# One-hot comparisons between the subtraction pieces, two batch tiles of pair products in a row, and the second layer of tile 2 moved ahead of the last pair products

## The reference, cut to what matters

```python
e = jnp.stack([tbl_0[ids[:, 0]], ..., tbl_25[ids[:, 25]]], axis=1)      # 512 x 26 x 128
combined = jnp.concatenate([e, r_dense_x[:, None, :]], axis=1)          # 512 x 27 x 128
interact = jnp.einsum('bfd,bgd->bfg', combined, combined)
z = interact[:, triu_i, triu_j]                                         # 512 x 351
h = jnp.concatenate([z, r_dense_x], axis=1)                             # 512 x 479
h = jnp.maximum(h @ W_top1 + b_top1, 0.0)                               # 512 x 512
h = jnp.maximum(h @ W_top2 + b_top2, 0.0)                               # 512 x 256
y = h @ W_top3                                                          # 512 x 1
```

## Time and profile before

| | |
|---|---|
| median of 3 runs | 109.18 us (109.17 to 109.2) |
| profiled execution | 109.18 us; span from its first to its last instruction 107.4 us |
| granted PE clock | 0.999 of full speed over the span |
| busy share of the span | PE 92%, DVE 74%, ACT 70%, POOL 62% |
| stretch 33.7 to 38.2 us, one turn of the one-hot loop | 4.50 us long: DVE busy 4.50, ACT busy 4.50, PE 4.45 |
| stretch 72.0 to 84.0 us, one batch tile | 12.00 us long: PE busy 12.00, DVE 7.61, ACT 6.42 |
| DMA, mean over the span | 108 GB/s; 343 to 398 GB/s from 18 to 24 us |

### The profile page before, as it was taken

How to read it: one execution, slowest core, us unless ns; L and a number is a source line. 1 busy time by engine, 2 the same in 40 slices (tenths; PEclk the granted TensorE clock), 3 DMA queues, 4 the chain that set the end, 5 groups by cost and what they waited for, 6 DMA issues and landing times.

```text
span 107.4 us, 2605 instructions
## 1 busy us (share of the span) xinstructions
PE 98.5 (92%) x998; PEld 79.0 (74%) x998; DVE 79.8 (74%) x162; ACT 75.0 (70%) x149; POOL 66.3 (62%) x72
## 2 busy tenths in 40 slices
PE   5999899989799999999798978999999989998992
PEld 1356676657467675887478958999999979997991
DVE  6599999999999999999943974588338922685120
ACT  4499999999999999999706842475527732474430
POOL 3777777777777787777877777777777750000000
PEclk9999999999999999999999999999999999999999
DMA  3852749995663636621211221221121220000000
GB/s 46 334 209 58 235 76 372 374 345 113 217 197 101 221 78 218 225 92 49 55 49 49 53 50 49 63 66 49 49 55 49 58 67 3 6 0 0 6 0 1
DMA packets 5200, 11.64 MB, mean 108 GB/s; under 512 B 1979, under 2 KB 2491, under 8 KB 5189
## 3 DMA queue, kind: packets, MB, share of 16 engines
q1 hardware_dynamic: 3120, 7.27, 21.2%
q0 software_dynamic: 2048, 4.20, 14.2%
q10 hardware_dynamic: 20, 0.02, 0.1%
HBM read 11.48 MB, written 0.00 MB: 107 GB/s over the span
## 4 chain that ended last, share of the span: by engine, by line
DVE 46%; PE 44%; issue 6%; ACT 2%; POOL 0%; DVEq 0%; POOLq 0%
DVE onehot L464 22%; PE gram_ps L613 13%; DVE low L476 13%; PE top_ps L678 5%; PE tr_ps L594 5%; PE act_ps L667 4%; PE dve_ps L667 4%; DVE onehot L470 3%; DVE xt L473 2%; PE gram_ps L578 2%; PE top_ps L702 2%; PE tr_ps L653 1%; DVE xt L450 1%; PE dve_ps L626 1%; PE act_ps L626 1%
## 5 line engine op out<-in xcount | busy, mean ns | idle before, releaser
L287 POOL DMA_INDIRECT rows<-table,ids_sb x64 | 65.5, 1023 | 20.8 <-issue 19.2
L578 PE MATMUL gram_ps<-onehot,high 128*128 128x512 f32 x82 | 23.1, 410 | 1.9 <-DVE onehot L464 1.6
L578 PE MATMUL gram_ps<-onehot,low 128*128 128x512 f32 x82 | 22.1, 411 | 0.0
L578 PEld LDWEIGHTS gram_ps<-onehot,high 128*128 128x128 f32 x82 | 14.3, 188 | 8.8 <-DVE onehot L464 5.0
L578 PEld LDWEIGHTS gram_ps<-onehot,low 128*128 128x128 f32 x82 | 15.4, 189 | 3.9
L464 DVE TENSOR_TENSOR onehot<-dve_ps,row_f 128x1024 fp32r<-128x1024 f32 (+1 forms) x10 | 14.4, 1479 | 1.2 <-PE act_ps L554 1.2
L464 DVE TENSOR_TENSOR onehot<-gram_ps,row_f 128x1536 fp32r<-128x1536 f32 (+1 forms) x10 | 14.9, 1531 | 0.0
L613 PE MATMUL gram_ps<-xt 128*58 128x52 f32 x512 | 14.5, 217 | 0.3 <-issue 0.3
L483 DVE COPY gram_sb<-gram_ps 26x208 f32<-26x208 f32 x32 | 12.0, 376 | 3.6 <-PE gram_ps L613 2.4
L613 PEld LDWEIGHTS gram_ps<-xt 128*58 128x58 f32 x512 | 14.0, 133 | 0.9 <-issue 0.5
L385 ACT ACTIVATE onehot<-onehot 128x1344 fp32r<-128x1344 f32 (+1 forms) x10 | 14.3, 1426 | 0.0
(11 more groups left out here) (83 smaller groups left out, 111.7 us busy)
## 6 DMA issues: line engine op xcount, KB each, us to landing
table<-table SPq DMA_DIRECT2D x9, 512.0 KB, 3.6
rows<-table,ids_sb POOLq DMA_INDIRECT x64, 2.9
w1p_sb<-w_pairs SPq DMA_DIRECT2D x1, 768.0 KB
table<-table SPq DMA_DIRECT2D x1, 640.0 KB, 3.8
w_sb<-w SPq DMA_DIRECT2D x1, 512.0 KB
dense_sb<-dense SPq DMA_DIRECT2D x1, 256.0 KB, 5.1
w1d_sb<-w_dense SPq DMA_DIRECT2D x1, 256.0 KB
ids_sb<-ids SPq DMA_DIRECT2D x1, 52.0 KB, 2.0
```

What stands on the lines that cost most here:

```text
L287: pool.indirect_dma_start(rows[:, t, s - 1, :], None, tables[f], bass.IndirectOffsetOnAxis(ids_sb[:, t, f:f + 1], 0)).then_inc(gathered[t] ...
L578: last = pe.matmul(pick_ps[b][:], weights[:, c, :], onehot[:, b, c, :], start=(c == 0 and part == 0), stop=(c == CHUNKS[o] - 1 and part == 1))
```

## The change

1. In the one-hot stage DVE's list is one turn ahead: between the four subtraction pieces of o stand the comparisons of o + 1. The three-chunk comparison is cut in two (`DVE_CHUNKS`), so a turn has one instruction more. The clears of `xt` for tiles 0 and 1 stand ahead of the first comparison, those for tiles 2 and 3 behind the one-hot stage.
2. `spread` from o = 2 on multiplies 10 rows instead of 128; the second of the two reads copies of its operands at partitions 32 to 41 (`select_again`, `ids_again`), which SP makes with two small transfers ahead of the table of o = 2.
3. Tiles 0 to 2 have four banks of four slots. The transposes of tile 0 stand behind the picks of o = 6 and o = 7, two banks of tile 1 behind those of o = 8, and the other two ahead of `gram(0)`.
4. The loop over t is written out: `gram(1)` comes right behind `gram(0)` and half of `dense_part(0)`. The banks of the pair products rotate over all tiles (`n % 3`).
5. `second_layer(2)` stands ahead of `gram(3)`, its two halves around the transpose of the last slot. It stood behind `gram(3)`.

```diff
-DVE_CHUNKS = {8: ((0, 1), (2, 3, 4)), 10: ((0, 1, 2), (3, 4, 5))}
+DVE_CHUNKS = {8: ((0, 1), (2,), (3, 4)), 10: ((0, 1, 2), (3,), (4, 5))}
...
+BANKS = [range(n, n + 4) for n in range(1, NG + 1, 4)]
+LAST_BANKS = BANKS[:-1] + [range(NG - 3, NG), range(NG, NG + 1)]
+BANK_SLOTS = [BANKS] * (TILES - 1) + [LAST_BANKS]
...
             for o, f in enumerate(ONEHOT):
+                if o == TABLES:
+                    sp.wait_ge(select_ready, 1)
+                    sp.dma_start(select_again[SPREAD_AT[1]:SPREAD_ROWS], select[0:NO]).then_inc(spread_again, 16)
+                    sp.wait_ge(ids16_ready, 1)
+                    sp.dma_start(ids_again[SPREAD_AT[1]:SPREAD_ROWS], field_ids16[0:NO]).then_inc(spread_again, 16)
                 if o >= TABLES:
                     sp.wait_ge(low_ready, REST * (o - TABLES + 1))
...
             for o in range(NO):
-                if o == NO - 1:
-                    transposed(0, (0, 1))
                 onehots(o)
...
+                if o == NO - 3:
+                    transposed(0, (1,))
+                if o == NO - 2:
+                    transposed(0, (3,))
...
             dve.tensor_copy(field_ids16[0:NO], field_ids[:]).then_inc(ids16_ready, 1)
+            for t in (0, 1):
+                dve.memset(xt[:, t, :, N_SLOTS:PAD], 0.0).then_inc(pad_zero, 1)
...
-                if o < TILES:
-                    dve.memset(xt[:, o, :, N_SLOTS:PAD], 0.0).then_inc(pad_zero, 1)
...
+            dve.wait_ge(ids_spread, 1)
+            whole_chunks(0, 0)
+            shared_chunk(0)
+            whole_chunks(0, 1)
+            whole_chunks(0, 2)
+            for o in range(NO - 1):
                 dve.wait_ge(high_ready, o + 1)
-                for c in rest_pieces(o):
-                    dve.tensor_tensor(low[:, b, c], table[:, o % TABLES, c], high[:, b, c].bitcast(F32),
-                                      ALU.subtract).then_inc(low_ready, 1)
+                rest(o, 0)
+                dve.wait_ge(ids_spread, o + 2)
+                if o >= 1:
+                    dve.wait_ge(pick_done, o)
+                whole_chunks(o + 1, 0)
+                if o == NO - 3:
+                    transposed(0, (0,))
+                if o == NO - 2:
+                    transposed(0, (2,))
+                rest(o, 1)
+                shared_chunk(o + 1)
+                rest(o, 2)
+                whole_chunks(o + 1, 1)
+                rest(o, 3)
+                whole_chunks(o + 1, 2)
...
+                pe.matmul(ids_ps_dve[o % 2][:], select[0:NO, o, :], field_ids16[0:NO, :], start=True, stop=True)
+                again = slice(SPREAD_AT[1], SPREAD_ROWS)
+                pe.matmul(ids_ps_act[o % 2], select_again[again, o, :], ids_again[again, :], start=True, stop=True
+                          ).then_inc(ids_spread, 1)
...
                 for s in range(SETS):
-                    if s >= GRAM_BANKS:
-                        pe.wait_ge(gram_out_act, t * SETS + s - GRAM_BANKS + 1)
-                        pe.wait_ge(gram_out_dve, t * SETS + s - GRAM_BANKS + 1)
+                    n = t * SETS + s
+                    if n >= GRAM_BANKS:
+                        pe.wait_ge(gram_out_act, n - GRAM_BANKS + 1)
+                        pe.wait_ge(gram_out_dve, n - GRAM_BANKS + 1)
...
             def back(t):
 
+                pe.wait_ge(gram_out_act, max(t + 1, 2) * SETS)
+                pe.wait_ge(gram_out_dve, max(t + 1, 2) * SETS)
                 pe.wait_ge(packed_act, t + 1)
...
+            gram(1)
+            transposes(2, (0, 1))
+            back(0)
+            dense_part(0, (2, 3))
+            first_layer(0, range(N1 // P))
+            transposes(2, (2,))
+            dense_part(1)
+            second_layer(0)
+            back(1)
+            transposes(2, (3,))
+            third_layer(0)
+            first_layer(1, range(N1 // P))
+            pe.wait_ge(pad_zero, TILES)
+            gram(2)
+            transposes(3, (0, 1))
+            dense_part(2)
+            second_layer(1)
+            back(2)
+            third_layer(1)
+            first_layer(2, (0, 2))
+            transposes(3, (2, 3))
+            first_layer(2, (1, 3))
+            second_layer(2, (0,))
+            transposes(3, (4,))
+            second_layer(2, (1,))
+            gram(3)
+            dense_part(3, (0, 2, 1, 3))
```

More of the change, by code:

```diff
@@ L67, with shared, act_cols @@
 NC = 3
+def shared(o):
+    return sum(len(cs) for cs in DVE_CHUNKS[CHUNKS[o]])
+def act_cols(o):
+    return (CHUNKS[o] - shared(o)) * B - SHARED_COLS[CHUNKS[o]]
 def rest_pieces(o):
@@ new lines, in shared_chunk, with rest @@
+            def shared_chunk(o):
+                c, cols = shared(o), SHARED_COLS[CHUNKS[o]]
+                dve.tensor_scalar(onehot[:, o % 2, c, 0:cols], ids_ps_dve[o % 2][:, 0:cols], row_f[:, c:c + 1], None,
+                                  ALU.is_equal).then_inc(onehot_dve, 1)
+            def rest(o, r):
+                b, piece = o % 2, rest_pieces(o)[r]
+                dve.tensor_tensor(low[:, b, piece], table[:, o % TABLES, piece], high[:, b, piece].bitcast(F32),
+                                  ALU.subtract).then_inc(low_ready, 1)
@@ L479, in gram @@
+            dve.wait_ge(high_ready, NO)
+            for r in range(REST):
+                rest(NO - 1, r)
             def gram(t, sets=range(SETS)):
@@ L555, in spread @@
                 last.then_inc(ids_spread, 1)
-            def pick(o, part):
-                b = o % 2
-                if part == 0:
-                    if o >= 2:
-                        pe.wait_ge(pick_out, o - 1)
-                    pe.wait_ge(high_ready, o + 1)
-                    weights = high[:, b]
-                else:
-                    weights = low[:, b]
-                for c in range(CHUNKS[o]):
-                    if part == 0:
-                        if c < shared(o):
-                            made = [c in cs for cs in DVE_CHUNKS[CHUNKS[o]]].index(True) + 1
-                        else:
-                            made = DVE_PARTS
-                            pe.wait_ge(onehot_act, o + 1)
-                        pe.wait_ge(onehot_dve, DVE_PARTS * o + made)
-                    elif c in [piece.start for piece in rest_pieces(o)]:
-                        pe.wait_ge(low_ready, REST * o + [piece.start for piece in rest_pieces(o)].index(c) + 1)
-                    last = pe.matmul(pick_ps[b][:], weights[:, c, :], onehot[:, b, c, :],
-                                     start=(c == 0 and part == 0), stop=(c == CHUNKS[o] - 1 and part == 1))
-                if part == 1:
-                    last.then_inc(pick_done, 1)
@@ L583, in transposes, with pick_low @@
+            def pick_low(o):
+                b = o % 2
+                for r, piece in enumerate(rest_pieces(o)):
+                    pe.wait_ge(low_ready, REST * o + r + 1)
+                    for c in range(piece.start, piece.stop):
+                        last = pe.matmul(pick_ps[b][:], low[:, b, c, :], onehot[:, b, c, :], start=False,
+                                         stop=(c == CHUNKS[o] - 1))
+                last.then_inc(pick_done, 1)
             def transposes(t, banks):
@@ L669, in first_layer, with second_layer @@
                     last.then_inc(h1_ready, 1)
-            def second_layer(t):
+            def second_layer(t, parts=range(N2 // P)):
                 if t:
@@ L675, in second_layer @@
                 pe.wait_ge(h1_out_dve, 2 * t + 2)
-                for m in range(N2 // P):
+                for m in parts:
                     for c in range(N1 // P):
@@ L765, in _ @@
-            second_layer(TILES - 2)
-            dense_part(TILES - 1, (0, 2, 1, 3))
-            for c in LAST_CHUNKS:
-                back_last(c)
+            pe.wait_ge(weights_in, WEIGHTS)
+            dense_part(0, (0, 1))
+            gram(1)
+            transposes(2, (0, 1))
[5 more added lines that the diff above has]
+            second_layer(0)
+            back(1)
+            transposes(2, (3,))
```

243 lines of the change are left out of this document (119 added, 124 removed).

## The result

The changed kernel took 111.53 us (median of 4 runs, 111.21 to 111.76) against 109.19 us before (109.17 to 109.2): the ratio is 1.0211, 95% interval 1.0199 to 1.0223. It is 2.1% slower; forecast were 108.7 us and a range to 109.8. The profiled execution took 111.21 us with a span of 109.3 us against 107.4. It is the fastest of the four, so of the 2.34 us its span shows 1.9; 0.1 lie outside the span and 0.32 between this execution and the median.

A forecast was written before the change was run, and what follows sets the result against it. ACT and DVE were taken to bound the one-hot stage, PE the tile stage. The span summed as 57.25 + 35.21 + 3.55 + 10.85 = 106.86 against 107.37, -0.5 us, giving 108.7 us; range 107.8 to 109.8.

The forecast's parts named there:

- Start to `gram(0)`: One-hot stage: `gram(0)` at 57.25 instead of 57.69 us, a gain of 0.44; bounds 56.6 to 57.9.
- between the ends: One-hot stage: ACT's loss at late tables taken as 0.55 us, between 0.33 (latency limits loads) and 0.8 (bandwidth).
- the forecast's bandwidth end: Table loads: if bandwidth limits the queue, the table of o = 4 lands 0.8 us later; ACT loses 0.8 in all.
- `gram(0)` to `gram(2)`: Tile stage: this stretch 1.42 us shorter, from eight transposes moved ahead (-1.02) and the changed waits.
- 1.88 us of old waits: Tile stage before, `gram(0)` to `gram(1)`: 10.31 us taken as 8.43 of work and 1.88 of waits.
- Second layer of tile 2: Ahead of `gram(3)`: +1.79 us of work and 0.70 + 0.10 of wait; the tail behind shrinks by 0.87.
- the value nothing: POOL's gathers: the last comes about 2.9 us sooner, single subtraction pieces holding them less; relief worth nothing.
- Small spreads: One-hot stage: paired small matmuls save some 0.2 us of PE a turn, but nothing is gained in the sum.
- its own bounds: Whole kernel: `gram(0)` at 56.6 to 57.9 and waits of 2.2 to 3.6 us, taken into the range 107.8 to 109.8.
- The signs: ACT idle only at o = 2 and 4, `gram(0)` near 57.2, PE waits 0.5 (`back(0)`) and 0.7 (second layer), among others.
- The slower rival: One-hot stage: later-issued table loads make ACT wait every turn, +1.9 us in all, 109.4 to 111; chance 0.18.

The follow-up runs named there:

- a_weights_last: Changed kernel with the layers' weights issued behind the last table (`WEIGHTS_AFTER = 9` instead of 3): 110.65 us, 1.0122 of the kernel before.
- b_second_ahead: Kernel before with only the second layer of tile 2 moved ahead of the last pair products: 111.27 us, 1.0193 of the kernel before.
- a_comps_first: Changed kernel with all comparisons of a field ahead of its four subtractions again, clears left moved: 110.39 us, 1.0137 of the kernel before.
- b_clears_moved: Kernel before with only the four clears of `xt` taken out of DVE's turns: 108.32 us, 0.9936 of the kernel before.
- a_wide_spread: Changed kernel with spreads multiplying all 128 rows again, the two small copies still made: 111.51 us, 1.0218 of the kernel before.
- b_clears_cols: Kernel before with clears moved and 32 columns of the shared one-hot chunk given from ACT to DVE: 108.1 us, 0.9891 of the kernel before.

## Why the prediction was wrong, point by point

- **Start to `gram(0)`: forecast -0.44, measured +0.80. This step failed.** Its mechanism was right: DVE's subtractions end at 11.05 and 15.58 (forecast 11.0 and 15.5), ACT loses 0.38 at o = 2 (forecast 0.33), then time at o = 4, then none. Two sizes were off. For ACT's loss at the tables the forecast took 0.55, "between the ends" 0.33 and 0.8; it was 1.18. SP's timeline of before has the weights and the table of o = 4 (the first of its six) issued at

```profile
15.02 0.43 SPq L262 DMA_DIRECT2D w1p_sb<-w_pairs  x1
...
19.73 23.25 SPq L257 DMA_DIRECT2D table<-table  x6
```

and that of the changed kernel:

```profile
15.99 0.43 SPq L272 DMA_DIRECT2D w1p_sb<-w_pairs  x1
...
20.14 25.31 SPq L267 DMA_DIRECT2D table<-table  x6
```

The table was issued 0.41 us later and ACT got it 1.18 later, more than even the 0.97 by which the weights ahead of it had moved. With 320 to 413 GB/s in each stretch from 18 to 25 us (343 to 398 before, up to 24), that is the forecast's bandwidth end and beyond it; a_weights_last, in which nothing is added at o = 4, agrees with that. What made the last 0.2 us is open. And the last fourteen picks behind ACT's part took 3.6 us (53.66 to 57.30), not 3.08.
- **`gram(0)` to `gram(2)`: forecast -1.42, measured -0.69.** The first waits came where forecast: `gram(1)` started 4.19 us after `gram(0)` (forecast 4.09) and `back(0)` 9.37 (forecast about 9.5). The gain was counted too high. The forecast got 1.88 us of old waits by subtraction, while PE's timeline of before names only these two between `gram(0)` and `gram(1)`:

```profile
63.95 0.52 PE L634 MATMUL gram_ps<-ident,packed 128*128 128x128 f32 x3 [0.79 <-DVE packed L498]
64.95 0.93 PE L667 MATMUL act_ps<-pairs_t,w1p_sb 128*128 128x128 f32 x6 [0.47 <-ACT pairs_t L320]
```

  It also left out a short wait: the third layer of tile 0 started at 76.30, right behind the results from ACT, which ended at 76.25. And eight transposes take 0.93 us from start to start (83.06 to 83.99 before), not 1.02. How the 0.73 divides among these was not separated.
- **Second layer of tile 2: right in kind and size.** The forecast had +1.79 of work and +0.80 of wait ahead of `gram(3)`, and -0.87 behind: +1.72. Measured +2.53 and -0.72. Part 5 alone costs 2.09 (b_second_ahead). A cost of 1.7 us was thus in the sum; it was outweighed there by gains of 0.44 and 1.42 in the first two stretches, and together these came to a loss of 0.11.
- **Gathers: the value nothing was right, its reason was wrong.** The last gather starts at 83.76, near the forecast 84, and nobody waits for it. But it does so with grouped subtractions too (83.92 in a_comps_first, where 86.7 was expected, and 83.71 in b_clears_moved). Single gathers are still held by the group there (POOL's timeline of a_comps_first):

```profile
17.16 1.72 POOL L297 DMA_INDIRECT rows<-table,ids_sb  x1 [0.30 <-issue]
...
83.92 0.94 POOL L297 DMA_INDIRECT rows<-table,ids_sb  x1 [0.30 <-issue]
```

  Before, three gathers of 1.25 us plus one hold of 0.72 made 4.47, DVE's own turn of 4.46, so that one gather of each turn fell into the subtractions; at ACT's turn of 4.57 they drift through. That is read from the starts, no run varied it alone. Nor do the traces tell what of a gather is held, the reading of its ids or the writing of its descriptors; the forecast took it for the second.
- **Small spreads: nothing**, as forecast (a_wide_spread), with hardly any of PE's time saved.
- **The range.** Every bound was set term by term and all four stretches missed to the same side, by 1.24, 0.73, 0.24 and 0.15. The upper ends of its own bounds (57.9 for `gram(0)`, 3.6 for the waits) add up to 110.1, so 109.8 was narrower than they were, and 111.53 lies beyond both.
- **The signs came true, the time did not.** ACT was idle only at o = 2 and o = 4, PE waited 0.80 ahead of the second layer of tile 2, and the last tile's first matmul came 3.1 after `gram(3)`. Only `gram(0)` at 58.49 instead of 57.2, and 0.22 instead of 0.5 ahead of `back(0)`, gave sign of a miss. The slower rival, a wait in every turn, did not happen either.

## What to carry to other kernels

Work that stands behind the last large block is not idle cargo: ask what runs under it. Moved ahead of the block it lengthened the path by its whole length and a wait (2.80 us for 1.79 of work), and gave back only the part that was not cover (0.76). When a producer's buffer is released by the last piece of a stage, spreading that stage over the next one delays the next load (here the table of o = 2, issued at 11.08 instead of 9.58); move the release, or add a buffer, first. And where two engines are both full, take the load off the one that costs nothing to relieve (here four clears, 0.87 us) before reordering anything.

## What the runs showed of the hardware that was not expected

Ten equal matmuls of 512 columns, queued behind the first spread, took between 2.38 and 3.88 us in the thirteen profiles that have ten (2.57, 2.61, 3.05 and 3.88 in b_clears_moved, before, the changed kernel and b_clears_cols). Their starts lie 0.43 us apart at first and 0.22 later, a ratio of two like that of the PE clock's levels, 1.2 and 2.4 GHz, and the change does not come at the same one of the ten in every profile. That the clock is the cause is a reading of this ratio: the row of the granted clock says 1.00 for these stretches. Up to the ten matmuls PE had done the same in all of them, four matmuls from 1.19 us on, a gap of 0.26 us, and the first spread.

The executions of the kernel before agree (109.15 to 109.37 over all that were timed), perhaps because its DVE compares with the second ids only from 9.47 us on. b_second_ahead, which has the same DVE list, scatters by 0.12 us, the other kernels with the ids behind the warm-up by 0.1 to 1.1. With the ids ahead of the warm-up the scatter was 0.09 us.
